# Splitting each attention's output earlier and on three engines, in a graph layer with a feed-forward block on one core

## The chip, the cores and the metric

One core of one Trainium2 chip runs the kernel. The metric is device microseconds (us) of one execution, the median of several; smaller is better. The engines of the core work side by side and wait for each other on semaphores: TensorE (PE in the profile) does the matmuls and transposes, VectorE (DVE), ScalarE (ACT) and GpSimd (POOL) do elementwise work, and SyncE (SP) issues the transfers.

## What is computed

`x` has 1250 rows of 512 values. A graph layer with 20000 edges is added to it first; then a feed-forward block, in which a router picks one spatial and one temporal expert, and three attentions of eight heads follow one another: the spatial one, the temporal one (causal), and the cross attention.

```
x = x + gnn(layernorm(x), edges)                 # two rounds of means over neighbours
z = layernorm(x)
s = attention(ln_s(z) @ Wq, ln_s(z) @ Wk, ln_s(z) @ Wv) @ Wo          # spatial expert
t = ln_t(z) + attention_causal(...) @ Wp                              # temporal expert
c = attention(s @ Wcq, t @ Wck, t @ Wcv) @ Wco                        # cross attention
y = z + c
x = x + y + gelu(ln_m(y) @ W1) @ W2
```

## The kernel before

**Numbers in two parts.** All arrays are float32. TensorE works on a rounded type (fp32r), so every operand A is split into hi(A), A rounded, and lo(A) = A - hi(A), and a product is three matmuls (`three`, L730 to L732): hi by hi, hi by lo, lo by hi. A split is thus two elementwise passes over SBUF, the second of which waits for the first. Weights come in units of 128 x 512 values; SyncE loads each into one of two buffers `w_raw`, and GpSimd splits it into one of four places of `w_hi` and `w_lo` (`cut_unit`, L583 and L598) once TensorE has done with the unit that was there four units earlier (`w_used`). SyncE loads a unit as soon as the unit two before it is split (`load_units`).

**Products.** `product_cols` computes one block of 128 output columns after the other for all 1250 rows: 4 blocks `m`, each of 4 blocks `k` of the contraction, each in three pieces of 512, 512 and 226 columns, 36 matmuls in all. Its blocks alternate between banks 0 to 2 and banks 3 to 5 of PSUM; block m+2 waits until block m has been read out (`free`). `product_rows` and `product_tile` compute row tiles of 125 rows by 512 columns.

**Attention.** `attend(K)` is called for `KS_` (spatial, turn 0), `KT_` (causal, turn 1) and `KC_` (cross, turn 2). Heads go in pairs; a head of turns 0 and 2 has ten steps, one of turn 1 five. In a step TensorE makes scores (L966, L967), VectorE their maximum (L1767), ScalarE the exponentials (L1173), TensorE transposes them (L981), ScalarE and VectorE split them (L1186, L1776), and TensorE multiplies them by the values (L1000). GpSimd splits the next head's queries, keys and values meanwhile (`cut_heads`). The output goes unnormalised to `ZT`, four blocks `ZT[:, k, :]` of 128 x 1250, one for each pair of heads. For each pair the inverse sums are split to `w_hi` and `w_lo`, TensorE spreads them over the partitions (L1016, `spread_inverses`, in three parts of 8, 8 and 4 matmuls), and VectorE multiplies (L1819, `normalise`). The spreads of the last pair stand alone at the end of an attention, in banks 7, 6 and 7, so that the third waits until the first has been read.

**After each attention** the output is split whole, as the operand `X1` of the next product: when all pairs are normalised, ScalarE writes hi of the four blocks (`cut_out`, L1156), VectorE lo (`cut_lo`, L1460), and TensorE begins the product with block k once lo of block k is there. `X1` lies over the split queries, keys and values (`QSH`, `QSL`, `KS`, `VS`) of the attention; in the kernel before its first two blocks lie over buffers of both heads of a pair. The three products are:

- turn 0, unit `qo`: the spatial output by a weight composed beforehand (`product_cols`), read out by ScalarE (L1346). Behind it comes the product `qt`, whose operand is the temporal norm. For it SyncE must first load `ZT` again from memory (L520), which waits until the last lo of turn 0 is made; VectorE applies the norm (L1469), ScalarE and VectorE split it, SyncE stores it, and only then does SyncE load the units of `qt`.
- turn 1, unit `ut`: VectorE reads out each block with the residual `XR` added (L1843), which SyncE loads at L538; in SyncE's queue that load stands behind the load of the fourth unit of `ut`, which waits until the second is split. Behind it stand a reload of 2.5 MB (L542) and the units of the next product, `kc`.
- turn 2, unit `uc`: the cross output by ten row tiles (`product_tile`), in banks 6 and 7 in turn. For each tile VectorE adds the residual row (`attended`, L1896), takes mean and variance, normalises it (`normed`, L1905); TensorE transposes it two tiles later (L1121), ScalarE reads that out (L1373), GpSimd makes hi (L719) and VectorE lo (`lo_tile`, L1911), three tiles behind `attended`. Then the MLP's first product starts (tile ranges of its pieces wait for lo of the tiles they need).

**GpSimd in turn 2.** After the last head it splits the first two units of `uc`, then makes ten residual rows (`residual_rows`, L638 and L641: normalise a row of 512 and add a bias), then waits for the last spread, splits the other two units of `uc`, does the ten hi tiles of L719, and then splits the MLP's units. Splits of `w_hi` places 2 and 3 wait for the last spread in every turn, since the inverse sums lie there.

## Time and profile before

| | us |
|---|---|
| median of 3 runs | 1731.62 |
| lowest and highest | 1729.80 and 1737.79 |
| the profiled execution's own time | 1727.27 |
| its span, first to last instruction | 1725.5 |

| engine | busy, us | share of the span |
|---|---|---|
| TensorE | 1596.2 | 93% |
| VectorE | 1148.8 | 67% |
| ScalarE | 879.1 | 51% |
| GpSimd | 734.6 | 43% |

Mean granted clock of TensorE: 0.974 of full. The profile is one execution; times in it are us from its first instruction. A row of the timeline gives the start, the duration, the engine, the line of the program and the operation, output <- input and how many instructions were merged into the row; in square brackets stands how long the engine had been idle before it and who released it. The three attentions end at about 735, 1045 and 1434 us, and the MLP's first product starts at about 1488.

### The profile page before, as it was taken

Reading aid. Unit: us, or ns where it says so; the run is one execution under the profiler, and the core shown is the slowest. Engines: PE = TensorE matmul, PEld = TensorE weight load, DVE = VectorE, ACT = ScalarE, POOL = GpSimd, SP = SyncE. Lnnn points to the kernel's source line nnn. Section 1 sums busy time; section 2 is a strip of 40 time slices with the busy share of each in tenths; the row PEclk is TensorE's granted clock in tenths of the full one; section 3 lists DMA queues with packets and bytes.
Section 4 is the critical chain, followed back from the end, with each engine's and each line's share of the span. In section 5 each row is a group of like instructions: output and inputs, shape, how many; then the busy total and the mean of one; then the engine's idle time right before and its main releaser. Section 6 shows DMA issues by size and latency. Waiting matters only on the chain.

```text
span 1725.5 us, 26353 instructions
## 1 busy us (share of the span) xinstructions
PE 1596.2 (93%) x9714; PEld 1355.3 (79%) x9714; DVE 1148.8 (67%) x1810; ACT 879.1 (51%) x1733; POOL 734.6 (43%) x596
## 2 busy tenths in 40 slices
PE   2788999699999999999999998999999997899997
PEld 1567877588788888878789996878888885678876
DVE  7998826720788988840288885168888887843323
ACT  3795313320788878732177772158878873301100
POOL 3120222145446545033568744363546465532430
PEclk9999999799999999989999998999999998899999
DMA  3000021333111112042222304302111210110111
GB/s 105 13 26 2 26 66 46 111 147 72 23 39 31 31 31 61 2 184 69 60 60 61 73 7 156 85 1 52 40 31 31 55 66 19 37 38 25 49 36 59
DMA packets 37347, 91.62 MB, mean 53 GB/s; under 512 B 6457, under 2 KB 8975, under 8 KB 36712
## 3 DMA queue, kind: packets, MB, share of 16 engines
q1 hardware_dynamic: 37224, 89.99, 18.9%
q8 instruction: 75, 1.23, 0.3%
q14 instruction: 48, 0.39, 0.1%
HBM read 45.40 MB, written 13.86 MB: 34 GB/s over the span
## 4 chain that ended last, share of the span: by engine, by line
PE 78%; DVE 8%; ACT 5%; POOL 4%; issue 3%; DMA 2%; DVEq 1%; SPq 0%; POOLq 0%; ACTq 0%
PE ps L1000 12%; PE ps L730 12%; PE ps L731 11%; PE ps L732 11%; PE ps L981 11%; PE ps L966 7%; PE ps L967 6%; DMA w_raw<-in_weights 1%; PE ps L925 1%; PE ps L926 1%; POOL F L638 1%; PE ps L1016 1%; ACT F L1173 1%; ACT F L1260 1%; DVE F L1568 1%
## 5 line engine op out<-in xcount | busy, mean ns | idle before, releaser
L1186 ACT ACTIVATE R<-ps 125x500 fp32r<-125x500 f32 (+3 forms) x632 | 291.8, 508 | 147.0 <-PE ps L981 145.6
L583 POOL TENSOR_TENSOR w_hi<-w_raw,zero 128x512 fp32r<-128x512 f32 x92 | 110.5, 1201 | 593.0 <-PE ps L732 282.4
L1767 DVE TENSOR_REDUCE TB<-ps 125x1 f32<-125x1250 f32 (+4 forms) x240 | 299.5, 1263 | 82.9 <-PE ps L967 56.5
L1776 DVE TENSOR_TENSOR R<-ps,R 125x500 fp32r<-125x500 f32 (+3 forms) x632 | 324.1, 569 | 12.9 <-ACT R L1186 12.9
L1173 ACT ACTIVATE F<-ps,TB 125x1250 f32<-125x1250 f32 (+4 forms) x240 | 276.1, 1157 | 60.2 <-DVE TB L1767 60.2
L1000 PE MATMUL ps<-R 125*128 125x252 f32 (+1 forms) x2080 | 288.9, 286 | 2.3 <-DVE F L1819 2.3
L981 PE MATMUL ps<-ident,F 125*125 125x125 f32 x2040 | 260.1, 275 | 9.6 <-ACT F L1173 8.5
L1000 PEld LDWEIGHTS ps<-R 125*128 125x128 f32 x2080 | 256.0, 189 | 2.6 <-DVE R L1776 1.6
L981 PEld LDWEIGHTS ps<-ident,F 125*125 125x125 f32 x2040 | 239.8, 189 | 12.9 <-ACT F L1173 12.4
L966 PE MATMUL ps<-R 128*125 128x512 f32 (+5 forms) x624 | 240.5, 386 | 5.1 <-DVE R L1776 4.0
L730 PE MATMUL ps<-R,w_hi 128*128 128x512 f32 (+3 forms) x576 | 212.1, 368 | 24.4 <-POOL w_lo L598 13.9
L967 PE MATMUL ps<-R 128*125 128x512 f32 (+5 forms) x624 | 218.3, 353 | 0.0
L583 POOL TENSOR_TENSOR R<-R,zero 128x1250 fp32r<-128x1250 f32 (+1 forms) x48 | 108.9, 2270 | 254.7 <-DMA R<-F 250.1
L731 PE MATMUL ps<-R,w_lo 128*128 128x512 f32 (+3 forms) x576 | 207.7, 361 | 0.0
L732 PE MATMUL ps<-R,w_hi 128*128 128x512 f32 (+3 forms) x576 | 207.4, 360 | 0.0
L730 PE MATMUL ps<-w_hi,R 128*125 128x512 f32 x440 | 180.0, 409 | 8.4 <-DVE R L1460 6.0
L966 PEld LDWEIGHTS ps<-R 128*125 128x125 f32 x624 | 115.9, 186 | 81.7 <-DVE R L1776 73.9
L731 PE MATMUL ps<-w_hi,R 128*125 128x512 f32 x440 | 175.2, 398 | 0.0
L732 PE MATMUL ps<-w_lo,R 128*125 128x512 f32 x440 | 174.7, 397 | 0.0
L730 PEld LDWEIGHTS ps<-R,w_hi 128*128 128x128 f32 x576 | 111.6, 194 | 43.2 <-POOL w_lo L598 14.4
L1491 DVE TENSOR_TENSOR F<-ps,brow 125x512 f32<-125x512 f32 x40 | 27.4, 692 | 175.2 <-PE ps L732 175.0
L598 POOL TENSOR_TENSOR w_lo<-w_raw,w_hi 128x512 fp32r<-128x512 f32 x92 | 132.2, 1437 | 7.2
(203 smaller groups left out, 2416.2 us busy)
## 6 DMA issues: line engine op xcount, KB each, us to landing
R<-F SPq DMA_DIRECT2D x96, 312.5 KB, 5.2
w_raw<-in_weights SPq DMA_DIRECT2D x88, 256.0 KB, 2.6
F<-in_weights SPq DMA_DIRECT2D x3, 1024.0 KB, 8.5
x_d<-F SPq DMA_DIRECT2D x10, 250.0 KB
zt_d<-F SPq DMA_DIRECT2D x1, 2500.0 KB, 14.0
F<-zt_d SPq DMA_DIRECT2D x1, 2500.0 KB, 9.3
xt_d<-F SPq DMA_DIRECT2D x4, 625.0 KB, 3.1
qc_d<-F SPq DMA_DIRECT2D x4, 625.0 KB, 5.7
```

The costliest lines, as they stand in the source:

```text
L583: return eng.tensor_tensor(to, a, zero[0:to.shape[0], :].to_broadcast(list(to.shape)), ALU.add)
L730: eng.matmul(to, ah, bh, start=first, stop=False)
L731: eng.matmul(to, al, bh, start=False, stop=False)
L732: return eng.matmul(to, ah, bl, start=False, stop=last)
L966: eng.matmul(piece, QSH[b][:, P * i:P * i + P], keys, start=True, stop=False)
L967: ins = eng.matmul(piece, QSL[b][:, P * i:P * i + P], keys, start=False, stop=not diagonal)
L981: ins = eng.transpose(ps[0:P, 3 * (n % 2) + bank, P * (j - j0):P * (j - j0) + P], PW[0:P, n % 2, P * j:P * j + P], ident[0:P, 0:P])
L1000: ins = eng.matmul(ps[:, pair_bank(m), to:to + width], VS[h % 2][:, c, :], probs(K, m, p, offset, width), start=start and p == 0, stop=sto ...
L1173: ins = eng.activation(PW[0:P, n % 2, P * first:P * first + P * blocks], flat(n % 2)[0:P, at:at + P * blocks], ACT.Exp, bias=ngm[0:P, 2 * ...
L1186: eng.activation(probs_run(K, n, 0, part, lo, hi), ps[0:P, 3 * (n % 2) + bank, P * (lo - j0):P * (hi - j0)] .rearrange("p (c t) -> p c t", ...
L1767: ins = eng.tensor_reduce(out=ngm[0:P, 2 * (n % 2) + part:2 * (n % 2) + part + 1], in_=flat(n % 2)[0:P, at:at + P * blocks], op=ALU.max, a ...
L1776: eng.tensor_tensor(probs_run(K, n, 1, part, lo, hi), ps[0:P, 3 * (n % 2) + bank, P * (lo - j0):P * (hi - j0)] .rearrange("p (c t) -> p c ...
```

## The change

- **Where a split lies.** `X1`'s blocks 0 and 1 now lie over buffers of the first head of a pair only, 2 and 3 over those of the second.
- **GpSimd** splits blocks 0 and 1 of the output (`cut_outputs`) behind the first weight units of the next product, as soon as the seventh head's scores (block 0) and its last values (block 1) are made, while the eighth head runs.
- **ScalarE** writes hi of block 2 once the last exponentials are out, and hi of block 3 in three parts, each behind its normalisation; **VectorE** makes lo of block 2 after the last normalisation, then lo of block 3 in three parts.
- **TensorE** does a first piece of the product (`begin_product`) ahead of the last pair's spreads, and the rest behind them (`continue_product`). The spreads go to banks 7, 6 and 5, and none waits for a normalisation. In turn 0 the product's block m=1 is begun beside m=0. In turn 2 the first four tiles are computed together in banks 0 to 3, and a tile's transposes follow four tiles later instead of two.
- **SyncE** waits for the parts instead of `cut_os`, loads the first two units of `uc` before the residual's input `XL` instead of after it, and `XL` in two halves.
- **GpSimd in turn 2** makes the residual rows in two halves: rows 0 to 4 after the output splits, rows 5 to 9 after the last two units of `uc`, in front of the hi tiles. Two of the MLP's units are split between the hi tiles.

```diff
-        QSH = [R[:, HB:HB + 1250], R[:, HB + 1250:HB + 2500]]
-        QSL = [R[:, HB + 2500:HB + 3750], R[:, HB + 3750:HB + 5000]]
+        QSH = [R[:, HB:HB + 1250], R[:, HB + 2500:HB + 3750]]
+        QSL = [R[:, HB + 1250:HB + 2500], R[:, HB + 3750:HB + 5000]]
...
@@ sync
-            eng.wait_ge(sp["os"].lo, KC)
+            eng.wait_ge(sp["os"].lo, KC - 2)
+            eng.wait_ge(ce.lo, 4)
             eng.wait_ge(zt_st, 16)
             eng.dma_start(ZT, zt_d).then_inc(zt_in, 16)
...
             load_row(4, ROWB["uc"])
+            load_units(UNIT["uc"], 2, C0 + 12)
             eng.wait_ge(A.cut, 39 * H)
-            eng.dma_start(XL[0:P], x1_d.rearrange("i p f -> p i f")).then_inc(xl_in, 16)
-            load_units(UNIT["uc"], 4, C0 + 12)
+            for lo, hi in ((0, HG), (HG, NT)):
+                eng.dma_start(XL[0:P, lo:hi, :], x1_d[lo:hi, :, :].rearrange("i p f -> p i f")).then_inc(xl_in, 16)
+            load_units(UNIT["uc"] + 2, 2, C0 + 14)
...
@@ gpsimd
+            def cut_outputs(K):
+
+                _, S = after_attention(K)
+                free = [(A.scores, K.super(7 * K.S - 1)), (A.pv, K.group(7 * K.G - 1))]
+                for k, (came, count) in enumerate(free):
+                    eng.wait_ge(came, count)
+                    eng.sem_inc(held, 1)
+                    eng.wait_ge(A.norm, 3 * (K.pairs0 + k + 1))
+                    hi_part(X1[0][:, k, :], ZT[:, k, :]).then_inc(S.hi, 1)
+                    eng.wait_ge(S.hi, k + 1)
+                    eng.tensor_tensor(X1[1][:, k, :], ZT[:, k, :], X1[0][:, k, :].bitcast(F32), ALU.subtract
+                                      ).then_inc(S.lo, 1)
...
                 cut_units(u, u + ahead(K))
+                cut_outputs(K)
                 if K.turn == 2:
-                    residual_rows()
+                    eng.wait_ge(A.cut, 39 * H)
+                    eng.wait_ge(row_in, 16 * 5)
+                    residual_rows(0, HG)
                 eng.wait_ge(A.bc, 3 * (K.pairs0 + H // 2))
...
             cut_units(UNIT["uc"] + ahead(KC_), UNIT["mlp"])
+            residual_rows(HG, NT)
+            eng.wait_ge(y_ready, NT)
+            eng.sem_inc(row_free, 1)
 
             for i in range(NT):
...
+                if i in (6, 8):
+                    cut_unit(UNIT["mlp"] + i // 2 - 3, i // 2 - 3)
+            cut_unit(UNIT["mlp"] + 2, 2)
+            cut_unit(UNIT["mlp"] + 3, 3)
...
@@ tensor
+            def begin_product(K):
+
+                unit, S = after_attention(K)
+                eng.wait_ge(w_split, 2 * unit + 2)
+                eng.wait_ge(S.lo, 1)
+                if K.turn < 2:
+                    cols_part(K, 0, 0)
+                else:
+                    for i in range(4):
+                        rows_part(i, 0)
+
+            def continue_product(K):
+
+                unit, S = after_attention(K)
+                for k in range(1, KC):
+                    if k < KC - 2:
+                        eng.wait_ge(S.lo, k + 1)
+                    elif k == KC - 2:
+                        if K.turn == 0:
+                            eng.wait_ge(w_split, 2 * unit + 4)
+                            for k1 in range(KC - 2):
+                                cols_part(K, 1, k1)
+                        eng.wait_ge(ce.lo, 4 * K.turn + 1)
+                    else:
+                        if K.turn == 0:
+                            cols_part(K, 1, KC - 2)
+                        eng.wait_ge(ce.lo, 4 * K.turn + 4)
...
+                begin_product(K)
                 eng.wait_ge(A.post, K.group(H * K.G - 1))
                 for j in range(3):
-                    if j:
-                        eng.wait_ge(A.norm, 3 * (K.pairs0 + H // 2 - 1) + j - 1)
-                    spread_inverses(K, H // 2 - 1, j, 7 - j % 2)
+                    spread_inverses(K, H // 2 - 1, j, 7 - j)
+                continue_product(K)
...
-            for i in range(NT + 2):
+            for i in range(4, NT + 4):
                 if i < NT:
-                    product_tile(pj["uc"], i, UNIT["uc"], X1, pj["uc"].v, ready=sp["oc"].lo)
-                if i >= 2:
-                    j = i - 2
+                    product_tile(pj["uc"], i, UNIT["uc"], X1, pj["uc"].v, since=6)
+                if i >= 4:
+                    j = i - 4
...
@@ scalar
+                eng.wait_ge(A.scores, K.super(K.N - 1))
+                eng.wait_ge(A.norm, 3 * (K.pairs0 + H // 2 - 1))
+                eng.activation(X1[0][:, KC - 2, :], ZT[:, KC - 2, :], ACT.Copy).then_inc(ce.hi, 1)
+                for j in range(3):
+                    eng.wait_ge(A.norm, 3 * (K.pairs0 + H // 2 - 1) + j + 1)
+                    eng.activation(X1[0][:, KC - 1, last_block(j)], ZT[:, KC - 1, last_block(j)], ACT.Copy
+                                   ).then_inc(ce.hi, 1)
...
@@ vector
                 for j in range(3):
-                    normalise(H // 2 - 1, j, 7 - j % 2)
+                    normalise(H // 2 - 1, j, 7 - j)
+                eng.wait_ge(ce.hi, 4 * K.turn + 1)
+                eng.tensor_tensor(X1[1][:, KC - 2, :], ZT[:, KC - 2, :], X1[0][:, KC - 2, :].bitcast(F32), ALU.subtract
+                                  ).then_inc(ce.lo, 1)
+                for j in range(3):
+                    last_lo(j)
```

TensorE at the end of the first attention, before. The rows of L1000 are the last values, those of L1016 the spreads of the last pair, those of L730 to L732 the product `qo`; in brackets stand the semaphores that a row waits for (`att_post`: output written, `att_norm`: normalised, `cut_os_lo`: lo of a block).

```order
L1000 MATMUL ps<-R 128x252 x19
L1016 MATMUL ps<-R,w_hi 128x126 [waits att_ilo,att_post]
...
L1016 MATMUL ps<-R,w_hi 128x126 [waits att_ilo,att_norm]
...
L1016 MATMUL ps<-R 128x126 [waits att_ilo,att_norm]
L1016 MATMUL ps<-R 128x126 x3
L730 MATMUL ps<-R,w_hi 128x512 [waits cut_os_lo,prod_qk_a,w_split]
```

The same place in the changed kernel, where L761 to L763 are the product, L1104 the spreads, and `cut_end_lo` is lo of blocks 2 and 3.

```order
L1088 MATMUL ps<-R 128x252 x19
L761 MATMUL ps<-R,w_hi 128x512 [waits cut_os_lo,w_split]
...
L1104 MATMUL ps<-R,w_hi 128x126 [waits att_ilo,att_post]
...
L1104 MATMUL ps<-R 128x126 [waits att_ilo]
L1104 MATMUL ps<-R 128x126 x3
L761 MATMUL ps<-R,w_hi 128x512 [waits cut_os_lo]
...
L761 MATMUL ps<-R,w_hi 128x226 [waits att_norm]
...
L761 MATMUL ps<-R,w_hi 128x512 [waits cut_end_lo]
```

Nine product matmuls have moved ahead of the spreads, and 27 more follow the spreads before the first wait for a block of the last two pairs.

GpSimd around the third attention's end, before: the first units of `uc`, the ten residual rows, the other units, the hi tiles.

```order
L598 TENSOR_TENSOR w_lo<-w_raw,w_hi 128x512 [waits w_split]
L638 TENSOR_SCALAR F<-F,mr 125x512 [waits xl_in,row_in,att_cut]
L641 TENSOR_TENSOR F<-F,brow 125x512 [waits y_norm]
...
L583 TENSOR_TENSOR w_hi<-w_raw,zero 128x512 [waits y_ready,w_used,w_in0,att_bc]
...
L719 TENSOR_TENSOR R<-F,zero 128x4x125 [waits lnm_ev] x10
```

The same in the changed kernel, where L595, L610 and L667 are the splits, L648 and L651 a residual row, L746 a hi tile, and `cut_oc_hi` is hi of a block of the output.

```order
L667 TENSOR_TENSOR R<-F,R 128x1250 [waits cut_oc_hi]
L648 TENSOR_SCALAR F<-F,mr 125x512 [waits xl_in,row_in,att_cut]
...
L595 TENSOR_TENSOR w_hi<-w_raw,zero 128x512 [waits w_used,w_in0,att_bc]
...
L648 TENSOR_SCALAR F<-F,mr 125x512 [waits xl_in]
...
L746 TENSOR_TENSOR R<-F,zero 128x4x125 [waits y_ready,lnm_ev]
L746 TENSOR_TENSOR R<-F,zero 128x4x125 [waits lnm_ev] x6
L595 TENSOR_TENSOR w_hi<-w_raw,zero 128x512 [waits w_used,w_in0]
...
L746 TENSOR_TENSOR R<-F,zero 128x4x125 [waits lnm_ev] x2
```

Five residual rows now stand between the last units of `uc` and the first hi tile, and the MLP's first unit ahead of the last three hi tiles.

## Rows read from the trace of the kernel before

**Rows 1.** The page, part 4: the chain that ended last, by engine.
```profile
PE 78%; DVE 8%; ACT 5%; POOL 4%; issue 3%; DMA 2%; DVEq 1%; SPq 0%; POOLq 0%; ACTq 0%
```

**Rows 2.** Timeline, TensorE at the first attention's end; columns as told above.
```profile
727.35 2.57 PE L1000 MATMUL ps<-R 125*128 125x252 f32 x20 [0.67 <-DVE F L1819]
731.14 0.33 PE L1016 MATMUL ps<-R,w_hi 125*128 125x126 f32 x1 [1.22 <-DVE F L1793]
...
738.32 0.76 PE L730 MATMUL ps<-R,w_hi 128*128 128x512 f32 x1 [3.94 <-DVE R L1460]
```

**Rows 3.** Stretches: length; busy PE, PEld, DVE, ACT, POOL; clock; DMA share; GB/s.
```profile
738.30:750.00 11.70, 11.68 (x48) 9.74 (x49) 6.17 (x5) 2.60 (x3) 3.15 (x2) 0.81 0.41 156
1048.50:1060.00 11.50, 11.50 (x46) 9.53 (x47) 8.21 (x4) 1.66 (x3) 7.68 (x4) 0.79 0.98 362
```

**Rows 4.** Timeline, the output's split after the first attention, and one later split alone.
```profile
734.94 4.66 ACT L1156 ACTIVATE R<-F 128x1250 fp32r<-128x1250 f32 x4 [4.61 <-DVE F L1819]
...
736.22 8.00 DVE L1460 TENSOR_TENSOR R<-F,R 128x1250 fp32r<-128x1250 f32 x4 [1.31 <-ACT R L1156]
...
755.83 1.46 DVE L1477 TENSOR_TENSOR R<-F,R 128x1250 fp32r<-128x1250 f32 x1 [0.48 <-ACT R L1339]
```

**Rows 5.** Timeline, from the product `qo` to `qt`: ScalarE, VectorE, GpSimd.
```profile
747.61 1.30 ACT L1346 ACTIVATE F<-ps,bcol_q 128x1250 f32<-128x1250 f32 x1 [8.01 <-PE ps L732]
...
768.35 1.30 ACT L1346 ACTIVATE F<-ps,bcol_q 128x1250 f32<-128x1250 f32 x1 [4.49 <-PE ps L732]
...
753.58 1.77 DVE L1469 TENSOR_SCALAR F<-F,lncol 128x1250 f32<-128x1250 f32 x2 [9.07 <-DMA F<-zt_d]
...
766.33 1.29 POOL L598 TENSOR_TENSOR w_lo<-w_raw,w_hi 128x512 fp32r<-128x512 f32 x1
```

**Rows 6.** Timeline at the second attention's end, and the transfer's time to landing.
```profile
1041.45 0.33 PE L1016 MATMUL ps<-R,w_hi 125*128 125x126 f32 x1 [3.24 <-DVE F L1793]
...
1048.45 0.77 PE L730 MATMUL ps<-R,w_hi 128*128 128x512 f32 x1 [3.93 <-DVE R L1460]
...
1058.02 1.52 DVE L1843 SCALAR_TENSOR_TENSOR F<-ps,ocol,F 128x1250 f32<-128x1250 f32 x1 [2.83 <-PE ps L732]
...
1047.61 0.36 SPq L538 DMA_DIRECT2D F<-xt_d  x1
...
F<-xt_d SPq DMA_DIRECT2D x1, 2500.0 KB, 9.6
...
1068.61 1.44 POOL L583 TENSOR_TENSOR w_hi<-w_raw,zero 128x512 fp32r<-128x512 f32 x1 [12.27 <-DMA w_raw<-in_weights]
```

**Rows 7.** Timeline at the third attention's end: TensorE and GpSimd.
```profile
1430.75 0.33 PE L1016 MATMUL ps<-R,w_hi 125*128 125x126 f32 x1 [2.29 <-DVE F L1793]
...
1401.69 2.08 POOL L638 TENSOR_SCALAR F<-F,mr 125x512 f32<-125x512 f32 x1
1403.85 1.27 POOL L641 TENSOR_TENSOR F<-F,brow 125x512 f32<-125x512 f32 x1
...
1396.93 1.04 POOL L583 TENSOR_TENSOR w_hi<-w_raw,zero 128x512 fp32r<-128x512 f32 x1 [19.28 <-DMA w_raw<-in_weights]
...
1441.59 2.26 POOL L583 TENSOR_TENSOR w_hi<-w_raw,zero 128x512 fp32r<-128x512 f32 x1
```

**Rows 8.** Timeline from the first hi tile to the MLP's first result.
```profile
1458.13 1.03 POOL L719 TENSOR_TENSOR R<-F,zero 128x500 fp32r<-128x500 f32 x1 [11.85 <-ACT F L1373]
...
1460.09 0.67 DVE L1911 TENSOR_TENSOR R<-F,R 128x500 fp32r<-128x500 f32 x1
...
1480.20 0.55 DVE L1905 TENSOR_SCALAR TB<-F,mv,sd 125x512 f32<-125x512 f32 x1
...
1472.67 1.48 ACT L1373 ACTIVATE F<-ps,lncol 128x125 f32<-128x125 f32 x4
...
1485.96 1.58 POOL L598 TENSOR_TENSOR w_lo<-w_raw,w_hi 128x512 fp32r<-128x512 f32 x1
...
1497.60 1.31 ACT L1383 ACTIVATE F<-ps,b1col 128x1250 f32<-128x1250 f32 x1 [12.87 <-PE ps L732]
```

More of the change, by code:

```diff
@@ L776, in product_part @@
+            def product_part(J, i, k, unit, X, free, n0=0, ready=None, k0=0, since=2):
+                if k == 0 and (not isinstance(n0, int) or n0 + i >= since):
                     eng.wait_ge(free, n0 + i - 1)
@@ L1105, in _ @@
             attend(KT_)
[L1106 removed]
+            product_cols(pj["u"], UNIT["ut"], X1, pj["u"].v, begin=1)
             product_cols(pj["qk"], UNIT["kc"], X0, pj["qk"].a, n0=20, k_ready=pj["u"].t,
```

74 lines of the change are left out of this document (46 added, 28 removed).

## The prediction

> **What bounds the kernel now.** I read the chain that ended last first: 78% of it is TensorE [rows 1]. So a change gains only where TensorE stands still or runs at its lower clock, and this change touches three such places, the ends of the attentions. I read TensorE's timeline there, then who released it. At the first, it ends the last values at 727.35 + 2.57 = 729.92, waits 1.22 for VectorE, makes 20 spreads until 738.32 - 3.94 = 734.38, and waits 3.94 for the first lo block [rows 2]. That is two elementwise passes in a row with nothing beside them: ScalarE's hi (4.66 for four blocks) and VectorE's lo (8.00 for four) [rows 4]. At the second the waits are 3.24 and 3.93 [rows 6], at the third 2.29 and then the product's start [rows 7]. The stretches right behind show a mean granted clock of 0.81 and 0.79 [rows 3]: part of them is at 1.2 instead of 2.4 GHz, after TensorE has hardly worked. Then I read what the next engine waits for behind each place, since there the gain can be taken back.
>
> **First attention.** GpSimd's new splits of blocks 0 and 1 cost it two passes each. It has nothing else to do there: it is idle from its last weight unit to the end of the spreads, and all that waits behind them (units 2 and 3 of `qo`) had to wait for the spreads anyway. I cost them at nothing. If that cover were gone, they would cost at most four passes of 2 to 3 us, and they begin some ten steps before the end. VectorE reads PSUM in most of its work there.
>
> TensorE's own work is unchanged. A block of `qo` takes (768.35 - 747.61) / 3 = 6.91 [rows 5]. The 20 spreads have half the columns of 20 matmuls of L1000, which took 2.57 [rows 2], so I take 2.4. From 729.92 on nothing need wait: 9 product matmuls (1.73) cover the 1.22; then the spreads to 734.1; then 27 matmuls (5.2) to 739.3, before any block of the last two pairs is asked for. VectorE has normalised by about 735.0 and owes two blocks of lo: 1.46 each alone, 2.00 each beside GpSimd [rows 4], so 737.9 to 739.3 with the three parts. Blocks m=0 and 1 are done at 729.92 + 2.4 + 2 x 6.91 = 746.1, against 747.61 + 6.91 = 754.5 before: **8.4 earlier**.
>
> Not all of it stays. `qt` needs its first unit split; before, that was ready at 766.33 + 1.29 = 767.6, and TensorE came to it at about 768.2, half a microsecond later [rows 5]. That unit hangs on a chain from the last lo: reload of `ZT` (744.22 to 753.58, 9.4), norm, stores, load, split. The last lo comes at 737.9 to 739.3 instead of 744.22, so the unit is ready at 761.3 to 762.7, while TensorE would be there at 759.8. A new wait of 1.5 to 2.9 appears, and the place gains 5.5 to 6.9. I take **6.0**, nearer the end with GpSimd and VectorE side by side. It also means that a clock that stays low a little costs nothing here.
>
> **Second attention.** TensorE is free at 1041.45 - 3.24 = 1038.2 [rows 6]; 1.7 of the 3.24 is filled. Spreads from 1041.4 to 1043.9, block k=1, then the wait for lo of blocks 2 and 3 (1047.8 to 1049): m=0 is done between 1049.7 and 1052.4 (the latter if the clock falls for a while, as it did), against 1057.8. But its reader L1843 needs the residual, which SyncE sends for at 1047.61 and which takes 9.6: 1057.2 [rows 6]. Before, that landed just ahead of the product and nobody saw it. It is sent when the second unit of `ut` is split, and that starts when the spreads are over: 0.6 earlier than now, with 0 to 2.3 more for splitting beside VectorE. So it lands at 1056.6 to 1058.9; read-out takes 1.52; block m=2, which needs its banks, starts at 1058.1 to 1060.4 against 1057.8 + 6.9 = 1064.7. The gain is 4.3 to 6.6; I take **5.7**. The units of `kc` land behind the same transfers, split at 1068.61 + 2.7 = 1071.3 [rows 6]; TensorE now comes at about 1072.8, so this is just not late.
>
> **Third attention.** TensorE ends the values at 1430.75 - 2.29 = 1428.5 [rows 7], does 12 product matmuls, spreads until 1433.7, 12 more, then waits for GpSimd to split two units. GpSimd is the engine to follow. It has made the first five residual rows before 1420 (L638 2.08 and L641 1.27, 3.42 with the gap [rows 7]; loading `uc` ahead of `XL` lets it start the splits early, which hides everything there). From 1433.7 it splits units 2 and 3: 4.7 alone, 9.2 beside VectorE (1.04 against 2.26 for the first pass [rows 7]); VectorE splits for some 4 us of it, so about 1440.9. Then come five rows, 17.1, to 1458.0, and only then the first hi tile, 1.03. VectorE, in order, makes three tiles and stands at `lo_tile(0)`, from about 1452 on. It gets on at 1459.1. Before, it made that lo at 1460.09 behind a hi of 1458.13 [rows 8]. So **the tile stage runs as before**: the head start of 5 us is eaten by rows 5 to 9. TensorE stands still for some 9 us meanwhile, so its tiles 6 and 7 run at the lower clock, and transposes follow four tiles behind: the last tile is normalised between 1 earlier and 2 later than 1480.20.
>
> What does move is the MLP's first unit. Before, it was ready after all hi tiles, 1485.96 + 1.58 = 1487.5 [rows 8]. Now it is split behind hi of tile 6; that tile is transposed only after tile 9's product, near 1477, and two read-outs of 1.48 [rows 8] and 2.3 of splitting give 1483.8. The first piece runs at the lower clock, the last piece waits for the last tile, and m=0 ends near 1493 to 1494 against 1497.4. I take **4.0**, with -3 (rows slowed, clock) and +9 (rows wholly hidden) as ends.
>
> **The sum.** 6.0 + 5.7 + 4.0 = 15.7. From the profiled execution's 1727.3 that is 1711.6; it lies 4.3 below the median of the runs, so against the median **1716**.
>
> **The Trainium skill on GpSimd beside VectorE.** The trace shows a GpSimd pass at 1.04 alone and 2.26 while VectorE ran L1460, an operation with two SBUF inputs, and L719 at 1.03 in the tile stage [rows 7, 8]. The Trainium skill, page "SBUF — State Buffer", section "SBUF: two separate sides", says that the port pair which the two share is an exclusive lock, taken by VectorE in a 2-port mode or with two SBUF inputs. By that rule rows 5 to 9, which lie beside additions from PSUM and statistics of one input, are hardly slowed. It speaks against the slower rival below; the row of L719 agrees. By its contrary the third term would be -13 instead of +4.
>
> **The rivals.** (a) *No gate holds*: the unit of `qt`, the residual of `ut` and the residual rows all arrive in time. Then 8.4, about 7.5 and 9: 25, so 1707. For it: TensorE is 78% of the chain. Against it: each gate has a row. 12%.
> (b) *The third place loses what it wins*: the low clock behind the 9 us of idleness, and the later transposes, put the last tile 3 to 5 later, and the MLP starts as before. Then 11.7 - 0 to 3: 1720 to 1723. 17%.
> (c) *GpSimd's second half at the contended rate*: a row takes 2.2 times its 3.4, five take 34 to 37 instead of 17. VectorE stands until about 1478, and the third place loses 17 to 20 against its 4: -13 to -16. With 11.7 from the other two that is 1 to 4 slower, 1733 to 1736. It decides from rows of 6.6 us on, where it eats all 15.7. L719's 1.03 speaks against it. 6%.
> (d) *TensorE's early piece is not early*: the seventh head's buffers come free too late, or GpSimd reaches the splits late, so that `begin_product` waits and the spreads behind it too. Then at most 2 to 5 of each place's gain stays: 1722 to 1729. Against it: the last ten steps take 35 us and four passes some 10. 5%.
> The forecast, 1711 to 1720, has 60%.
>
> **How the numbers follow.** About 0.5%, 8.7 us, is what a measurement of this kernel can tell from no change. Faster by more than that (below 1723): forecast, (a), most of (b), together 0.83 of the chance with a deduction for an unseen wait. Within it: the rest of (b), (d): 0.12. Slower: (c) with something unknown, which needs a further 5 us: 0.05. The range 1706 to 1725 leaves out (c), half of (d), and little else; the terms' own ends (5.5 to 6.9, 4.3 to 6.6, -3 to 9) give 1709 to 1725 by themselves, and the runs scatter by 8.
>
> **What would show it.** Right: no wait of TensorE over 1 us between last values and the end of `qo`, m=1; a wait of 1.5 to 3 before `qt` released by GpSimd's w_lo; L1843's successor starting on a transfer near 1057 less the gain before it; the first hi tile right behind the tenth residual row, and VectorE idle for 6 to 8 before its first lo tile. Wrong: a lower clock through `qo`; TensorE waiting for a block of GpSimd's; residual rows over 4 us in the second half; the MLP's first product starting before 1470 or after 1485 in the old kernel's count.

## The result, and the profile after

The changed kernel takes 1724.61 us (median of 20 runs, 1721.73 to 1729.85), the kernel before 1730.53 (20 runs, 1727.50 to 1740.15). The ratio is 0.9961, with a 95% interval of 0.9951 to 0.9972: faster by about 6 us, 0.4%. I had forecast 15.7 us, 1716.

The profiled execution of the changed kernel has an own time of 1724.62 and a span of 1722.8. The chain that ended last has hardly another shape than in [rows 1]:

```profile
PE 78%; DVE 10%; ACT 6%; issue 3%; POOL 2%; DMA 1%; DVEq 0%; SPq 0%; ACTq 0%; POOLq 0%
```

**How the two traces are set side by side.** The last values of the first attention start at 730.02 in this trace and at 727.35 in the one of before [rows 2], and nearly all of this difference is there before anything that the change touches: that attention's first values start at 450.9 and 448.3. In the runs below the row of the last values lies between 728.1 and 732.9. So I measure from one attention's last values (the last row of values before the spreads of the last pair) to the next one's. "Place 1" is from there in the first attention to the second attention, place 2 to the third, place 3 to the end of the span. Since code is shifted, line numbers differ by a few between the runs.

| | place 1 | place 2 | place 3 |
|---|---|---|---|
| before | 308.85 | 389.69 | 299.61 |
| changed | 306.57 | 386.24 | 299.97 |
| changed, mean of all profiles in which this place is as changed (6, 6 and 5 of them) | 305.8 | 386.7 | 300.4 |
| forecast of the gain | 6.0 | 5.7 | 4.0 |
| gain, by the means | 3.1 | 3.0 | -0.8 |

Profiles of one form of a place differ by up to 1.3 (by 1.6 in place 3 of e5 and e8 below), and of the kernel before there is one profile, so each gain is known to about 1. Part of the scatter is TensorE's clock: some 100 us into place 2 it is lower for a while in e2, e3, e5 and e6 (387.1 to 387.3), and not in the changed kernel, e1 and e4 (386.2 to 386.3).

**Place 1.** TensorE in the changed kernel: the last values, the first wait worth naming, and the first matmul of `qt`.

```profile
730.02 2.57 PE L1088 MATMUL ps<-R 125*128 125x252 f32 x20 [0.67 <-DVE F L1906]
...
756.35 0.46 PE L761 MATMUL ps<-R,w_hi 128*128 128x512 f32 x1 [0.66 <-ACT F L1435]
...
766.56 0.79 PE L761 MATMUL ps<-R,w_hi 128*128 128x512 f32 x1 [3.05 <-POOL w_lo L610]
```

The waits of 1.22 and 3.94 of [rows 2] are gone, as forecast. In their place stands 3.05 before `qt`. VectorE and GpSimd show where it is made: L1930 is lo of block 2, L1925 the three parts of lo of block 3, L1556 the norm behind the reload of `ZT`; L595 and L610 are the splits of the third and fourth unit of `qo`.

```profile
737.10 1.86 DVE L1930 TENSOR_TENSOR R<-F,R 128x1250 fp32r<-128x1250 f32 x1
738.88 4.63 DVE L1925 TENSOR_TENSOR R<-F,R 128x500 fp32r<-128x500 f32 x3
...
752.79 1.77 DVE L1556 TENSOR_SCALAR F<-F,lncol 128x1250 f32<-128x1250 f32 x2 [9.01 <-DMA F<-zt_d]
```

```profile
736.60 1.04 POOL L595 TENSOR_TENSOR w_hi<-w_raw,zero 128x512 fp32r<-128x512 f32 x1 [31.78 <-PE ps L1104]
737.71 2.39 POOL L610 TENSOR_TENSOR w_lo<-w_raw,w_hi 128x512 fp32r<-128x512 f32 x1
740.07 1.47 POOL L595 TENSOR_TENSOR w_hi<-w_raw,zero 128x512 fp32r<-128x512 f32 x1
741.62 1.61 POOL L610 TENSOR_TENSOR w_lo<-w_raw,w_hi 128x512 fp32r<-128x512 f32 x1
```

Three short operations (the row merges two of 128 x 500 and one of 128 x 250) take 4.63, as long as GpSimd's passes beside them; the last, with half the elements, takes 1.50 by itself, and the first 1.77. The last lo comes 10.9 after the last values' end (743.51 - 732.59); before it was 14.3, and I had taken 8.0 to 9.4. And in this profile the wait costs more than it lasts. Stretches of the changed kernel (columns as in [rows 3]): `qo`, then the 18 matmuls behind the wait, then two stretches of place 2.

```profile
738.00:750.00 12.00, 12.00 (x63) 10.14 (x63) 5.75 (x6) 1.31 (x1) 5.15 (x3) 1.00 0.46 175
...
766.50:772.90 6.40, 6.34 (x18) 5.18 (x19) 0.00 (x0) 0.00 (x0) 5.63 (x6) 0.51 0.54 198
...
1052.00:1056.00 4.00, 4.00 (x14) 3.29 (x13) 0.00 (x0) 0.00 (x0) 1.42 (x2) 0.58 0.99 419
1056.00:1062.00 6.00, 6.00 (x33) 5.08 (x33) 2.38 (x2) 1.26 (x1) 0.00 (x0) 0.99 1.02 286
```

The clock, 0.81 through `qo` before, is 1.00 there now. But behind the new wait it is at the lower level: 18 matmuls take 6.4 instead of 3.5 (12 at 0.23 and 6 at 0.11, their distance at full clock).

That is the longest low stretch of the six profiles in which place 1 is as changed. All six wait before `qt`, for 2.99 to 3.39, but the same 6.40 behind the wait hold 18 matmuls here, 24 in e3 and 32 in e5, where the clock does not fall at all (below, the stretch of e3, then the end of the wait and the stretch of e5):

```profile
766.40:772.80 6.40, 6.35 (x24) 5.23 (x25) 0.00 (x0) 0.00 (x0) 5.62 (x5) 0.73 0.55 207
```

```profile
766.26 0.50 PE L761 MATMUL ps<-R,w_hi 128*128 128x512 f32 x1 [3.07 <-POOL w_lo L610]
...
766.20:772.60 6.40, 6.34 (x32) 5.35 (x33) 0.00 (x0) 0.00 (x0) 5.53 (x6) 1.00 0.60 191
```

The first 36 matmuls of `qt` take 9.8 in the changed kernel's profile, 8.6 in e3, e4, e6 and e7, and 7.0 in e5. So the low clock costs 2.8, 1.6 or nothing there.

**Place 2.** TensorE, then VectorE's first read-out of `ut`:

```profile
1041.84 0.33 PE L1104 MATMUL ps<-R,w_hi 125*128 125x126 f32 x1 [1.47 <-DVE F L1880]
...
1046.78 0.50 PE L761 MATMUL ps<-R,w_hi 128*128 128x512 f32 x1 [0.70 <-DVE R L1930]
...
1051.29 0.50 PE L761 MATMUL ps<-R,w_hi 128*128 128x512 f32 x1 [2.53 <-DVE R L1925]
```

```profile
1058.30 1.52 DVE L1939 SCALAR_TENSOR_TENSOR F<-ps,ocol,F 128x1250 f32<-128x1250 f32 x1 [7.06 <-DMA F<-xt_d]
```

The same slow lo stands in front of block k=3, again with a low clock behind it (0.58). The read-out does start on the residual's landing, as I had forecast.

**Place 3.** The row of GpSimd is the first hi tile, the second VectorE's first lo tile, the third TensorE's product of tile 6, the last the MLP's first matmul.

```profile
1454.74 2.00 POOL L746 TENSOR_TENSOR R<-F,zero 128x500 fp32r<-128x500 f32 x2 [0.18 <-POOL F L651]
```

```profile
1455.80 1.48 DVE L2004 TENSOR_TENSOR R<-F,R 128x500 fp32r<-128x500 f32 x1 [7.92 <-POOL R L746]
```

```profile
1457.93 0.79 PE L761 MATMUL ps<-w_hi,R 128*125 128x512 f32 x1 [10.98 <-DVE F L1989]
...
1483.48 1.10 PE L1209 MATMUL ps<-ident,TB 125*128 125x125 f32 x4 [1.73 <-DVE TB L1998]
1484.23 0.78 PE L761 MATMUL ps<-R,w_hi 128*128 128x512 f32 x1
```

The third attention's last values are 3.06 earlier here than before (1422.83 against 1425.89). Put back by that, the first lo tile stands at 1458.9 (I had said 1459.1), but the MLP's first matmul at 1487.3, where it was before (1487.59), and the read-out of its first block at 1493.87 + 3.06 = 1496.9 against 1497.60 [rows 8].

### The profile page after: what moved, and what is told of

Read it like the earlier page. It is cut to its first block, busy times and chain, and to the rows that moved or that the text cites. A ratio compares the mean times of both kernels' runs of the same rounds, so it can differ in the third digit from the quotient of the medians.

```text
span 1722.8 us, 26353 instructions
## 1 busy us (share of the span) xinstructions
PE 1595.9 (93%) x9714; PEld 1354.1 (79%) x9714; DVE 1140.0 (66%) x1810; ACT 872.8 (51%) x1733; POOL 744.8 (43%) x608
## 4 chain that ended last, share of the span: by engine, by line
PE 78%; DVE 10%; ACT 6%; issue 3%; POOL 2%; DMA 1%; DVEq 0%; SPq 0%; ACTq 0%; POOLq 0%
PE ps L1088 14%; PE ps L1069 13%; PE ps L761 10%; PE ps L762 10%; PE ps L763 10%; PE ps L1054 8%; PE ps L1055 6%; ACT F L1355 1%; PE ps L1013 1%; PE ps L1014 1%; PE ps L1104 1%; ACT F L1364 1%; ACT F L1261 1%; PE ps L948 1%; ACT R L1274 1%
## 5 line engine op out<-in xcount | busy, mean ns | idle before, releaser
L595 POOL TENSOR_TENSOR w_hi<-w_raw,zero 128x512 fp32r<-128x512 f32 x92 | 107.0, 1163 | 560.5 <-PE ps L763 281.5
L761 PE MATMUL ps<-R,w_hi 128*128 128x512 f32 (+3 forms) x576 | 212.8, 370 | 17.8 <-POOL w_lo L610 11.2
L595 POOL TENSOR_TENSOR R<-R,zero 128x1250 fp32r<-128x1250 f32 (+1 forms) x48 | 108.8, 2267 | 263.9 <-DMA R<-F 259.6
L763 PE MATMUL ps<-R,w_hi 128*128 128x512 f32 (+3 forms) x576 | 208.0, 361 | 0.0
L761 PE MATMUL ps<-w_hi,R 128*125 128x512 f32 x440 | 179.7, 408 | 14.4 <-DVE F L1989 11.8
L763 PE MATMUL ps<-w_lo,R 128*125 128x512 f32 x440 | 174.6, 397 | 0.0
L761 PEld LDWEIGHTS ps<-R,w_hi 128*128 128x128 f32 x576 | 111.8, 194 | 36.5 <-POOL w_lo L610 11.5
L610 POOL TENSOR_TENSOR w_lo<-w_raw,w_hi 128x512 fp32r<-128x512 f32 x92 | 129.4, 1407 | 7.2
```

Of the source, the lines that this page charges most:

```text
L595: return eng.tensor_tensor(to, a, zero[0:to.shape[0], :].to_broadcast(list(to.shape)), ALU.add)
L761: eng.matmul(to, ah, bh, start=first, stop=False)
L763: return eng.matmul(to, ah, bl, start=False, stop=last)
```

## Experiments

Each is the changed kernel with an edit, timed beside the kernel before. Places in us, as above; bold where the edit touches.

| run | ratio to before, 95% interval | place 1 | place 2 | place 3 |
|---|---|---|---|---|
| changed | 0.9961, 0.9951 to 0.9972 | 306.57 | 386.24 | 299.97 |
| e1 reload in parts | 0.9924, 0.9911 to 0.9938 | **300.39** | 386.33 | 300.53 |
| e2 splits behind lo | 0.9933, 0.9920 to 0.9947 | **301.50** | 387.13 | 300.77 |
| e3 residual early | 0.9957, 0.9943 to 0.9972 | 305.57 | **387.08** | 300.46 |
| e4 nine rows first | 0.9905, 0.9889 to 0.9920 | 305.34 | 386.30 | **290.00** |
| e5 and sums later | 0.9889, 0.9871 to 0.9908 | 305.96 | 387.17 | **287.75** |
| e6 nine rows, two behind | 0.9887, 0.9870 to 0.9904 | 305.29 | 387.27 | **287.59** |
| e7 second place | 0.9936, 0.9921 to 0.9950 | 305.80 | **382.11** | 300.47 |
| e8 all gates | 0.9849, 0.9833 to 0.9865 | **300.49** | **382.20** | **289.34** |
| e9 no early piece | 0.9962, 0.9948 to 0.9975 | **306.94** | **387.57** | **299.10** |
| e10 all, two behind | 0.9839, 0.9825 to 0.9852 | **300.53** | **382.62** | **287.76** |

**e1: the reload of `ZT` in three parts.**

```diff
-            eng.wait_ge(sp["os"].lo, KC - 2)
-            eng.wait_ge(ce.lo, 4)
             eng.wait_ge(zt_st, 16)
-            eng.dma_start(ZT, zt_d).then_inc(zt_in, 16)
+            for came, count, lo, hi in ((sp["os"].lo, KC - 2, 0, KC - 2), (ce.lo, 1, KC - 2, KC - 1), (ce.lo, 4, KC - 1, KC)):
+                eng.wait_ge(came, count)
+                eng.dma_start(ZT[:, lo:hi, :], zt_d[:, lo:hi, :]).then_inc(zt_ins[max(lo - 1, 0)][0], 16)
```

> The changed kernel, but SyncE reloads ZT for qt in three parts: blocks 0 and 1 as soon as GpSimd has split them (long before the attention's end), block 2 behind its lo, block 3 behind the last lo; VectorE waits for the part that it needs. Theory: in the first attention the changed kernel gives back most of its head start at one point. TensorE waits 3.05 for the first unit of qt, which hangs on the reload (issued at 743.57, landed 9.2 later), and behind that wait 18 matmuls go at half the clock (766.5 to 772.9, granted clock 0.51: 6.4 instead of 3.5). If so the wait and the slow stretch both vanish: 3.05 + 2.9 = 5.9 us, ratio to the kernel before 0.9961 - 0.0034 = 0.993. Rival 1, the slow stretch is there whatever TensorE waits: only 3.05 comes back, 0.9943. Rival 2, the unit's chain behind the reload (norm, stores, load) is bound by something else than the landing of the last part: the wait stays above 2, 0.996.

The last lo is as slow as ever (4.62 for three parts), but VectorE makes the norm of blocks 0 and 1 at once, 742.79 instead of 752.79. TensorE shows no wait over 0.3 between the last values and 800, and the clock stays up; e1's stretches:

```profile
760.00:766.00 6.00, 6.00 (x37) 5.24 (x36) 0.00 (x0) 1.30 (x1) 5.44 (x5) 1.00 0.31 96
766.00:772.00 6.00, 6.00 (x30) 4.98 (x29) 0.00 (x0) 0.00 (x0) 2.56 (x3) 1.00 1.02 416
```

The place is 5.4 shorter than in the mean of the others, near the 5.9 of the theory, and rivals 1 and 2 fall: 3.05 alone would have given 302.7. But the theory's two terms are not what was won. Counted from the last values to the second attention's first exponentials, which leaves out what comes later in the place, it is 119.8 in e1 and 125.8 in the mean of the six as changed, 6.0 more, and still 125.1 in e5, whose clock stayed up. So 5.3 is the gate without any low clock: the wait of some 3.1, one of 0.6 to 0.7 for ScalarE's read-out, in e5 one of 0.83 for the bias of `qt` (see e2), and about 0.8 that I can't place. The low clock adds nothing in e5, 0.4 to 0.8 in e3, e4, e6 and e7 and 1.7 in the changed kernel's profile.

**e2: GpSimd's splits behind the lo.**

```diff
             cut_heads(KS_)
+            eng.wait_ge(ce.lo, 4)
             cut_units(UNIT["qo"] + ahead(KS_), UNIT["ut"])
```

> The changed kernel, but in the first attention GpSimd splits the third and fourth unit of qo only when VectorE has made all parts of lo. Theory: the three parts of lo of block 3 take 4.63 together because GpSimd works beside them (each part ends with one of its passes); alone they take about 0.7 each, 2.0 to 2.3 together, so the last lo comes 2.3 to 2.6 earlier against the last values, and the reload of ZT and the first unit of qt with it. The wait before qt falls from 3.05 to 0.5 to 0.8, and the clock behind it stays up: 2.3 + 2.9 = 5 us, ratio 0.993. If the clock goes down behind a short wait too, 0.9947. Rival: the parts are slow by themselves (a short operation with a wait on ScalarE in front of each): still 4.6 for three, GpSimd's units only later, TensorE waits for the third unit, ratio 0.996 to 0.998.

VectorE in e2, the same three parts:

```profile
738.24 1.59 DVE L1926 TENSOR_TENSOR R<-F,R 128x500 fp32r<-128x500 f32 x3
```

1.59 instead of 4.63: the parts were slow only beside GpSimd (the first 0.67 instead of 1.77, the last 0.41 instead of 1.50). The wait before `qt` is 0.56, with a clock of 1.00 around it, and the place is 4.3 shorter. That is 1.1 less than in e1, 1.9 less if counted to the first exponentials (121.7 against 119.8): 0.56 is that wait, and the next follows: TensorE waits 0.82 at 777.91, where block m=2 of `qt` needs m=0 read out, and ScalarE makes that read-out only at 776.46, after 12.71 of idleness put down to the bias of `qt` (`bcol_q`), which VectorE scales once its load, late in SyncE's queue, has landed. The trace puts TensorE's 0.82 down to a GpSimd pass that ends at the same time, but that one splits the first unit of `kt`, which block m=2 does not need; its own unit was split by 768.1.

**e3: the residual sent early.**

```diff
-            load_units(UNIT["ut"], 4, e_t * 16 + (T0 + 12))
+            load_units(UNIT["ut"], 2, e_t * 16 + (T0 + 12))
             eng.wait_ge(A.cut, 26 * H)
...
             eng.dma_start(XR, xt_d).then_inc(xr_in, 16)
+            load_units(UNIT["ut"] + 2, 2, e_t * 16 + (T0 + 14))
```

> The changed kernel, but SyncE sends the reload of the residual XR for ut right behind the loads of the first two units of ut, ahead of the other two. My prediction held this transfer to be what bounds the second place (VectorE's first read-out of ut starts on its landing, with 7.06 of idleness). Theory now: it does not bound it, since TensorE has block m=1 to do until 1062 and the first read-out, 1058.3 + 1.5 = 1059.8, is there before block m=2 asks for it; what cost there is the 2.53 wait for the last lo and the clock behind it (0.58 from 1052 to 1056). So: the read-out starts near 1055, TensorE's rows move by less than 0.5, ratio 0.996. Rival, the prediction's gate: the gain is 2 to 3 us, ratio 0.9945.

VectorE's first read-out of `ut` in e3, and TensorE's wait for the last lo:

```profile
1053.06 1.52 DVE L1940 SCALAR_TENSOR_TENSOR F<-ps,ocol,F 128x1250 f32<-128x1250 f32 x1 [3.14 <-PE ps L764]
```

```profile
1049.97 0.50 PE L762 MATMUL ps<-R,w_hi 128*128 128x512 f32 x1 [2.53 <-DVE R L1926]
```

The read-out is now released by TensorE and comes 3.9 sooner against the last values (17.8 behind them instead of 21.7), and place 2 is not shorter: 387.08 against 386.7, or against 387.1 to 387.3 in the profiles with the same late stretch of low clock. The transfer that I had named as the gate was not one.

**e7: the second place's lo freed.**

```diff
             cut_heads(KT_)
+            eng.wait_ge(ce.lo, 8)
             cut_units(UNIT["ut"] + ahead(KT_), UNIT["uc"])
```

with the edit of e3 as well.

> The changed kernel, but in the second attention GpSimd splits the second to fourth unit of ut only behind the last part of lo, and the reload of XR is sent ahead of the third unit's load (else it would go out later still). Theory: the last lo is then there 2.6 to 3 earlier against the last spread (three parts in 1.6 instead of 4.6), TensorE's 2.53 wait for it goes, and so does the low clock behind it (some 1.2 us of it): 3 to 3.7 us, ratio 0.9961 - 0.002 = 0.994, granted clock 1.0 from 1048 to 1062. Rival: GpSimd's splits, now later by 3, make TensorE wait for the second unit of ut instead: same, 0.9955 to 0.9965.

```profile
1048.37 1.59 DVE L1927 TENSOR_TENSOR R<-F,R 128x500 fp32r<-128x500 f32 x3
```

```profile
1043.97 0.33 PE L1106 MATMUL ps<-R,w_hi 125*128 125x126 f32 x1 [1.47 <-DVE F L1882]
...
1048.50 0.50 PE L763 MATMUL ps<-R,w_hi 128*128 128x512 f32 x1 [0.32 <-DVE R L1932]
...
1052.55 0.51 PE L763 MATMUL ps<-R,w_hi 128*128 128x512 f32 x1 [0.35 <-POOL w_lo L611]
```

The parts take 1.59, TensorE's 2.53 is gone, and the later splits cost 0.35. The granted clock is 1.00 in every stretch from 1048 to 1074. Place 2 is 4.6 shorter than the mean, 4.2 than the profiles that have no late stretch of low clock either; both are more than the 3 to 3.7 expected. With e3 as its control the gain belongs to the lo and the clock. e3's edit was needed as a part of this one and brought nothing alone.

**e4: nine residual rows first.**

```diff
-                    residual_rows(0, HG)
+                    residual_rows(0, 9)
...
-            residual_rows(HG, NT)
+            residual_rows(9, NT)
```

> The changed kernel, but GpSimd makes nine of the ten residual rows in its idle time during the last heads, and one behind the last two units of uc. Theory: rows 5 to 9 (1437.08 to 1454.6) are what holds the first hi tile, VectorE behind it (7.92 at lo_tile) and TensorE behind that (10.98, then 0.51 of the clock until 1462.5). With four of them gone from there the first hi tile comes near 1444 to 1446, the wait of 10.98 falls to 1 to 3, the low clock goes, and the MLP's first product starts 6 to 9 earlier: ratio 0.996 - 0.004 = 0.991 to 0.993. Rival 1, the tile stage is bound by its own chain (a transpose four tiles behind, read-out, hi, lo): it starts earlier but runs slower, and less than 3 us reach the end, 0.9945 or more. Rival 2, VectorE's twenty sums in front of the MLP's split eat what arrives: the second product of the MLP starts no more than 1 earlier, 0.996.

TensorE, then ScalarE's read-outs of the MLP's first four blocks in e4:

```profile
1445.97 0.50 PE L761 MATMUL ps<-w_hi,R 128*125 128x512 f32 x1 [2.09 <-DVE F L1989]
...
1453.48 0.50 PE L761 MATMUL ps<-w_hi,R 128*125 128x512 f32 x1 [0.77 <-DVE F L1989]
```

```profile
1478.63 1.30 ACT L1470 ACTIVATE F<-ps,b1col 128x1250 f32<-128x1250 f32 x1 [5.10 <-PE ps L763]
1485.56 1.31 ACT L1470 ACTIVATE F<-ps,b1col 128x1250 f32<-128x1250 f32 x1 [5.63 <-PE ps L763]
1499.71 1.31 ACT L1470 ACTIVATE F<-ps,b1col 128x1250 f32<-128x1250 f32 x1 [12.84 <-DVE R L2032]
1502.64 1.31 ACT L1470 ACTIVATE F<-ps,b1col 128x1250 f32<-128x1250 f32 x1 [1.63 <-DVE R L2032]
```

The 10.98 is 2.09 (its clock stays at 1.00), and place 3 is 10.4 shorter, a little more than the 6 to 9 expected. The first read-out comes 12.2 earlier against the last values than in the changed kernel (58.8 instead of 71.0); 10.4 reach the end. Rival 1 falls; rival 2 has 1.8 of it.

**e5: VectorE's twenty sums behind the MLP's split**, on e4.

```diff
-            for i in range(NT):
-                if i == NT - 1:
-                    eng.wait_ge(acc_ok, 1)
-                eng.tensor_tensor(ACC[0:P, i, :], YL[0:P, i, :], XL[0:P, i, :], ALU.add).then_inc(acc_ok, 1)
...
+            def first_sums():
...
+                if isinstance(q, int):
+                    first_sums()
                 for i in range(NT):
                     eng.wait_ge(J2.ps, NT * q + i + 1)
```

> Nine residual rows first, as in the run before, and VectorE's twenty sums into the output rows stand behind its split of the MLP's first four blocks instead of ahead of it. Theory: with the MLP started early these sums (13.04 + 8.06) are what comes next. There the third gelu waits 12.84 for VectorE, and of the 12.2 us that the first gelu had won against the changed kernel 10.5 reached the first sum behind the second product. Without them in front all 12.2 should: 1.7 us better than with the nine rows alone, ratio 0.9905 - 0.001 = 0.9895, the third and fourth gelu released by TensorE 6.9 apart. Rival: the second product was held by TensorE's own work alone, so that nothing moves, or the sums, now between split and read-outs, hold those up and cost 2 to 5: 0.9905 to 0.993.

```profile
1496.54 1.30 ACT L1470 ACTIVATE F<-ps,b1col 128x1250 f32<-128x1250 f32 x1 [5.63 <-PE ps L763]
1503.47 1.31 ACT L1470 ACTIVATE F<-ps,b1col 128x1250 f32<-128x1250 f32 x1 [5.63 <-PE ps L763]
```

The third and fourth read-out are released by TensorE, 6.93 apart. By the profiles place 3 is 2.25 shorter than in e4; e8, which has the same place 3, has 289.34, only 0.7 shorter, and the ratios (0.9889 and 0.9905) have intervals that overlap. So the order of the read-outs is shown, its worth only to about 1.5.

**e6: transposes two tiles behind**, on e4.

```diff
-            for i in range(4, NT + 4):
+            for i in range(4, NT + 2):
...
-                if i >= 4:
-                    j = i - 4
+                for j in (range(3) if i == 4 else [i - 2]):
```

> Nine residual rows first, and a tile's transposes follow two tiles later, as in the kernel before, instead of four. The question is whether the four tiles of distance make the tile stage slower. Theory: with them the last four tiles' transposes stand behind the last product: 9 tiles after the product's end at 1460.2 TensorE does nothing but transposes and waits 1.5 + 3.35 + 1.7, and hi and lo of the last tiles come late. Two behind, hi of tile 6 and with it the MLP's first unit come 2 to 3 earlier, and the first gelu 1 to 3 earlier: ratio 0.9905 - 0.001 = 0.9895 (0.989 to 0.9905). Rival: VectorE is busy for 84 to 87 of 100 there and sets the pace of the last tiles (attended, statistics, normed, lo: 3.4 to 4 us a tile), whichever way the transposes stand: no change, 0.9905, or a loss since TensorE waits earlier.

TensorE's last transposes in e4 and in e6:

```profile
1462.79 0.65 PE L1209 MATMUL ps<-ident,TB 125*128 125x125 f32 x4 [1.51 <-DVE TB L1998]
...
1466.78 1.09 PE L1209 MATMUL ps<-ident,TB 125*128 125x125 f32 x4 [3.35 <-DVE TB L1998]
...
1469.60 1.10 PE L1209 MATMUL ps<-ident,TB 125*128 125x125 f32 x4 [1.73 <-DVE TB L1998]
```

```profile
1468.56 0.65 PE L1208 MATMUL ps<-ident,TB 125*128 125x125 f32 x4 [1.97 <-DVE TB L1997]
...
1471.38 1.10 PE L1208 MATMUL ps<-ident,TB 125*128 125x125 f32 x4 [2.18 <-DVE TB L1997]
```

Place 3 is 2.4 shorter, and the MLP's first matmul stands 49.1 behind the last values' start instead of 50.6. The ratios of e4 and e6 have intervals that overlap, so of these 2.4 some 1.5 are seen at the MLP's start and the rest is within the scatter.

**e8 and e10: all of it.** e8 joins e1, e3 with e7, e4 and e5; e10 adds e6.

> All of it together on the changed kernel: reload of ZT in parts, splits behind the lo in the second attention with XR early, nine residual rows first, the sums behind the MLP's split. If the places are independent, their gains add: 5.9 or a little over (first place, ratio by 0.0037), 3.3 (second, 0.002), 9.6 + 1.7 (third, 0.0066): 20.5 us under the changed kernel, ratio 0.9961 - 0.012 = 0.984, about 1703 to 1705. Rival: a gate behind one of them is shared (SyncE's queue, or GpSimd's time), so that 4 us or more of the sum are missing: 0.9865.

> All gates taken away as in the run with all of it, and the transposes two tiles behind. Theory: the transposes' distance and the sums are independent (each alone made the third place 2.3 shorter, 290.0 to 287.7 from its last values to the end): 300.5, 382.2 and 285.5 to 288 in the three places, ratio 0.9849 - 0.001 = 0.984, about 1704. Rival: the sums being gone, VectorE's time in the tile stage no longer shows, and the distance is worth nothing: 0.985.

e8 is at 1706.52 (1704.11 to 1708.57), e10 at 1703.44 (1701.46 to 1706.54), against 1732.88 and 1731.36 of the kernel before beside them. The ratio of e8, 0.9849, is nearer its theory (0.984) than its rival (0.9865, the end of its interval). Places 1 and 2 are within about half a microsecond of what e1 and e7 had. Place 3 is 289.34 in e8 and 287.76 in e10, where e5 had 287.75 without the shorter distance. So the distance and the sums, 2.4 and 2.25 each alone, aren't shown to add: the rival of e10 is as good as its theory there. e10 beats both kernels, by 27.9 and about 21 us.

**e9: without TensorE's early piece.**

```diff
-                begin_product(K)
                 eng.wait_ge(A.post, K.group(H * K.G - 1))
                 for j in range(3):
                     spread_inverses(K, H // 2 - 1, j, 7 - j)
+                begin_product(K)
                 continue_product(K)
```

> The changed kernel, but in all three attentions TensorE does the first piece of the product (block k=0) behind the last pair's spreads, not ahead of them; all splits stay where the change put them. Theory: in the changed kernel a later gate takes back whatever the piece wins, and long waits cost more than their length. In the first place the product then reaches qt 1.7 later, the wait there shrinks from 3.05 to about 1.3, and if the clock stays up behind so short a wait, up to 2.9 us are gained. In the second the wait for the last lo shrinks from 2.53 to 0.8, with up to 1.2 us of low clock less. In the third the 10.98 wait absorbs all. From the last values of one attention to the next: 303 to 306 (305.8 in the mean of the runs with an unchanged first place), 385.5 to 387, 300 to 300.5; ratio 0.993 to 0.9965. Rival, the prediction's view that TensorE's idle time in front of the spreads is what counts: 1.2 to 1.7 lost in each place, 307.3, 388.3, 301.5, ratio 0.9985.

TensorE in e9 at the first matmul of `qt`, and at the spreads of place 2 with the stretch around them:

```profile
765.52 0.50 PE L761 MATMUL ps<-R,w_hi 128*128 128x512 f32 x1 [0.20 <-POOL w_lo L610]
```

```profile
1040.28 0.33 PE L1104 MATMUL ps<-R,w_hi 125*128 125x126 f32 x1 [3.24 <-DVE F L1880]
```

```profile
1040.00:1048.00 8.00, 7.72 (x31) 7.07 (x32) 4.84 (x6) 1.63 (x3) 3.20 (x2) 0.57 0.00 0
```

Against the means of the changed kernel the places are 1.2 and 0.8 longer and 1.3 shorter; the ratio is the same, 0.9962. The wait before `qt` is 0.20 and the clock 1.00 there, so the theory's mechanism is seen, but not its gain: the spreads of place 2 stand behind 3.24 and run at the lower clock, those of place 1 behind 1.24 do too (0.52 from 733.0 to 739.5), and at `qt` TensorE waits 0.99 at block m=2, as in e2. In place 3 the spreads start 1.4 earlier, and the first lo tile, which waits for GpSimd behind them, comes 1.1 earlier. So as changed the early piece is worth about nothing in all: 1.2 and 0.8 in its favour and 1.3 against it are hardly beyond the scatter.

## Why the prediction was wrong

The size was off by more than half: 15.7 forecast, about 6 measured.

**What was right.** TensorE shows no wait over 1 us between the last values and the end of `qo`, m=1, and the clock is up there. The waits of [rows 2] and [rows 6] are gone or smaller. A wait before `qt` released by GpSimd's w_lo came as said, and the first lo tile came within 0.2 of where it was put. Residual rows 5 to 9 took 3.4 to 3.6 each, so rival (c) did not come. The gains without gates were right too: from the last values to the second attention's first exponentials it is 128.2 before and 119.8 in e1, 8.4 less, as worked out for rival (a); place 2 is 7.5 shorter in e8, as said there.

**Place 1: two steps of the sum.** (1) "2.00 each beside GpSimd [rows 4], so 737.9 to 739.3 with the three parts". I priced block 3's lo by its elements. It is three operations, and each ended only behind one of GpSimd's passes: 1.54 each in the mean instead of 0.53 (e2). The last lo came 1.5 to 2.9 later than that, and the wait was 3.05 instead of 1.5 to 2.9 (TensorE came 1.0 later than forecast as well, or it would have been longer). The Trainium skill, page "SBUF — State Buffer", section "SBUF: two separate sides", which I had used for the residual rows alone, says of the port pair that "whichever ... starts first gets the pair for the whole instruction; the other fully blocks". By that rule the count of operations sets the price. e2 agrees, and so do the sizes: beside GpSimd the 128 x 250 took 1.50 instead of 0.41, the 128 x 1250 of block 2 took 1.86 instead of 1.45. (2) "It also means that a clock that stays low a little costs nothing here". That looked at `qo`, and at nothing behind the gate. At `qt` 4.3 of the 8.4 were left, at the second attention 1.4 (128.22 against 126.86) in the changed kernel's profile, where the wait that I had forecast had 2.9 us of low clock behind it. In the five other profiles of this form 2.3 to 3.1 were left, 3.1 in e5, where the clock stayed up: there the lost 1.2 is mostly the next gate, the bias of `qt` (0.83). So behind `qt` the next gate or the low clock took 1.2 to 2.9 that my sum did not have. e1 gives back nearly all of it, e2 less, since TensorE still waits for the bias.

**Place 2: the wrong gate.** "Its reader L1843 needs the residual": true, and of no effect, since TensorE had block m=1 to do until 1061.6 and m=0's read-out was over at 1059.8, in the changed kernel; e3, where it comes 3.9 sooner, wins nothing. What counted was again the last lo (1046.65 + 4.59 = 1051.24, or 1050.9 in the old count, instead of 1047.8 to 1049), the wait of 2.53 for it and the low clock behind it: m=1 took 8.1 instead of 6.9. e7 takes both away for 4.6. I had priced that lo by its elements here too.

**Place 3: the right gate, and two missing steps behind it.** The rows ate the head start, as said. But the MLP started at 1487.3 in the old count, later than the 1485 that I had named as a sign of being wrong. It does not start when its unit is split (1481.7 here): its matmuls stand in TensorE's queue behind the last transposes, and these wait for the last `normed`, 1482.36. That one came 3.2 behind the late end of the 1479.2 to 1482.2 forecast (1485.4 in the old count): VectorE had stood still for 7.92, TensorE ran at 0.56 of the clock from 1457 to 1463, and transposes followed four tiles behind (1.5 to 2.4 by e6, measured where the rows were not in the way). Then I had said nothing of the twenty sums of VectorE; the first read-out's 0.7 was gone at the MLP's second product (1522.70 + 3.06 = 1525.8 against 1525.40 before). So the 4.0 became about zero: rival (b) came in this place, and I had given it 17% as if the other two were sure.

**The chances.** I gave 0.83 to faster by over 0.5%; it was 0.4%. The range, up to 1725, just holds the time. I had taken the middle of each place's bounds and let them make up for each other; but all three errors point one way, since a gate that is reached too early costs its wait, and behind it the next gate or the clock.

## What to carry to other kernels

When a change lets the bottleneck engine arrive earlier at a gate, the new wait takes back its length, and behind it the next gate or a stretch of low clock takes more: in place 1, of a head start of 8.4, a wait of 3.0 to 3.4 and what hung on it took 6.0 in the mean of six profiles, and 5.3 in the one whose clock stayed up. Look for what the gate hangs on (a reload that can go in parts, rows that can be made in idle time): the edits of e10 were worth 21 us where the change itself brought 6. Count VectorE's operations, not their elements, where GpSimd works on SBUF beside them.
